# Macaron block on one core: paired slots in the first FFN, a shorter first stage, earlier scatters, and the last tables spread over half slots

## The chip, the cores and the metric

The kernel runs on one core of a Trainium2 chip. The metric is the device time of one execution in microseconds (us). Three timed executions of the kernel before gave 701.39, 701.4 and 705.12 us, with a median of 701.4 us. The profile is of one more execution.

## The reference

The input is x of shape (2, 2048, 256), so T = 4096 rows of D = 256, all float32. Three residual steps follow each other:

```
x = x + 0.5 * ffn(layernorm(x))
x = x + attn(layernorm(x))          # three gated linear recurrences, width 64, then up to 256
x = x + 0.5 * ffn(layernorm(x))     # the same weights again

def ffn(x, Wr, br, ln_g, ln_b, W1, b1, W2, b2):      # E = 8 experts, F = 1024
    logits = x @ Wr + br
    gate = max(softmax(logits)); idx = argmax(logits)     # one expert per row
    xn = layernorm(x) * ln_g + ln_b
    h = relu(xn @ W1[idx] + b1[idx])                      # 256 -> 1024
    return (h @ W2[idx] + b2[idx]) * gate                 # 1024 -> 256
```

Which rows go to which expert depends on the data. With the reference's router on its inputs (seed 0) the first FFN sends 332, 17, 1583, 15, 1969, 2, 0 and 178 rows to experts 0 to 7.

## The kernel before

**Slots.** Each FFN routes its rows: every row is written by an indirect DMA (a scatter, L743, GpSimd) into the region of its expert in DRAM (`routed_rows`), and is later read back in tiles of 128 rows of one expert. A tile is a slot. The work of a slot is: load 128 rows (`slot_rows`, SyncE) and the expert's W1 (`weights`, 1 MB); normalise on VectorE (`norm`, L1337); transpose on TensorE (`turn_input`, L1907); scale and shift on ScalarE (`affine`, L1626); first product (`first_product`, L1935, 16 products that the profile lists as 32 matmuls); bias and ReLU, half on ScalarE (L1654), half on VectorE (`activate`, L1369); second product (`second_product`, L1969, 16 matmuls listed); bias, gate and residual on VectorE (`finish`, L1387 and L1394); scatter of the result to its rows (`store`, L752, GpSimd).

**Software pipeline.** In the turn of slot i TensorE transposes slot i+1, runs the first product of slot i, then the second product of slot i-1. The order is written out by hand and is static. Two waits matter here. The second product of slot i-1 waits until VectorE has read all earlier second products, so on `finish(i-2)` (`m_yk`). The second half of the first product of slot i waits until VectorE has run `activate(i-1)` (`m_a`).

**Tables and stages.** Slot numbers are turned into row addresses and experts by tables that VectorE computes with small operations (`tables`, parts 0 to 5, after the counts of a quarter of the rows have come in). An FFN is cut into stages, so that it starts before all rows are routed. The first FFN has a stage of FULL = 9 slots (full tiles from the first half of the rows) and a second stage with all the rest. The second FFN has stages of 4, 9, 9 slots and the rest. A static number of slots, FIXED = 32, always runs; the ones behind that run under an `If` on the number of slots in use (`slots_used`). SLOTS = 39 is the upper bound in the first FFN.

**Paired slots.** A pair slot holds 64 rows of each of two experts (`is_pair`). The second FFN has three, at slots 24, 27 and 30; the first FFN has none. A pair needs two W1 loads and a second W2 (`pair_second_weights`, 1 MB into `w2_b`), has its first product the other way round (L1926), copies it out (L1349), transposes it back (`turn_hidden`, L1947), activates after that (`activate_pair`, L1357) and has a second product in two halves (L1961, L1963). VectorE chooses the experts (`pairs`, parts 0 to 2): experts with an odd number of half tiles come first.

**Work beside the slots.** Everything else (routing of the later quarters, tables, layer norms, the recurrences) stands in lists of positions k at the top of the file. Slot i has a place, `PLACE[p][i]`; in the first FFN that is i, plus 1 from the second stage on. `beside(at)` of VectorE, ScalarE and GpSimd runs what stands at k from 48*place to 48*place+23 ahead of the slot's activation, and at 48*place+24 to 48*place+47 behind it. For TensorE a place has 192 positions, in eight parts between the quarters of the products. Places go up to 39 in the first FFN whether or not a slot is in use: the work beside them is issued either way. `beside` work that is placed at slots 35 to 38 (places 36 to 39) is the first recurrence layer of the third quarter, the end of the recurrence of the second quarter (`up`, `add_recurrence` L1284, `moments` L856) and `turn_logits`. Chunk c of x is read back from `x_middle` (`load_x`) at slots 17, 23, 31 and after the last one (`WITH`).

**Engine order.** Each engine runs its own instructions in order. SyncE issues all loads in order: W1 of slot i+3, then rows of slot i+4; at a stage's first slot it waits for that stage's table (`s_tab`) and for the scatters.

## Time and profile before

| | |
|---|---|
| median of 3 timed executions | 701.4 us |
| profiled execution, its own time | 700.31 us |
| its span in the trace | 698.5 us |
| TensorE matmul busy | 642.4 us (92%) |
| VectorE busy | 412.0 us (59%) |
| ScalarE busy | 268.1 us (38%) |
| GpSimd busy | 168.6 us (24%) |
| slots run, first and second FFN | 37 and 34 (three of these are pairs) |

Busy time is the sum of an engine's spans; the share is of the span. The time that counts is that of the engine that the others wait for at each stretch, and that is read from the gaps ("idle before") and from what ended them.

### The profile page before, as it was taken

What the parts mean: (1) busy time and instruction counts of PE and PEld (TensorE: products, weight loads), DVE (VectorE), ACT (ScalarE), POOL (GpSimd) and SP (SyncE); (2) the same over time, 40 slices, a digit from 0 to 9 for tenths busy, and PEclk for the clock granted to TensorE, in tenths of its full rate; (3) what the DMA queues carried; (4) which work ended last, traced back from release to release, by engine and by line L of the source; (5) the groups of instructions that cost most, each with busy time, mean ns of one, the idle gap of its engine ahead of it and who ended that gap; (6) DMA issues with size and microseconds to landing.
All of it is one profiled execution on the core that took longest, in us unless ns stands there. A gap on an engine that the chain in (4) does not pass through costs nothing.

```text
span 698.5 us, 15261 instructions
## 1 busy us (share of the span) xinstructions
PE 642.4 (92%) x4294; PEld 550.9 (79%) x4294; DVE 412.0 (59%) x1446; ACT 268.1 (38%) x639; POOL 168.6 (24%) x174
## 2 busy tenths in 40 slices
PE   7549999999999999999998998999979899999993
PEld 5448988999988878898677867879878888786782
DVE  7756673333356586777787684877756762344331
ACT  4204221323245557553571644744442311233220
POOL 4633433111121120133312341104411331111111
PEclk9659999999999999999998999999999999999998
DMA  8969876845464463436415436434274445767640
GB/s 284 315 206 388 276 255 207 275 166 203 161 205 147 156 204 107 134 128 189 168 55 198 147 117 223 137 98 153 87 260 145 132 173 192 236 210 257 235 151 18
DMA packets 62512, 129.25 MB, mean 185 GB/s; under 512 B 8010, under 2 KB 39253, under 8 KB 62293
## 3 DMA queue, kind: packets, MB, share of 16 engines
q1 hardware_dynamic: 55940, 111.25, 47.8%
q0 software_dynamic: 6480, 16.92, 6.6%
q8 instruction: 41, 0.67, 0.4%
q14 instruction: 51, 0.41, 0.2%
HBM read 109.10 MB, written 19.96 MB: 185 GB/s over the span
## 4 chain that ended last, share of the span: by engine, by line
PE 63%; DVE 15%; issue 8%; DVEq 6%; POOL 3%; DMA 2%; ACT 1%; POOLq 0%; ACTq 0%; SPq 0%
PE bank L1935 27%; PE bank L1969 24%; PE bank L1907 2%; DVE st L856 2%; POOL routed_rows L743 2%; DVEq L454 2%; PE bank L1926 2%; PE bank L1961 2%; DVE rec L1253 1%; DVE act_t L1369 1%; DVE y_b L1387 1%; PE bank L1824 1%; DVE rec L1229 1%; PE bank L1831 1%; PE bank L1762 1%
## 5 line engine op out<-in xcount | busy, mean ns | idle before, releaser
L1935 PE MATMUL bank<-mn_t,w 128*128 128x128 f32 x2176 | 268.4, 280 | 8.3 <-DVE act_t L1369 4.7
L1935 PEld LDWEIGHTS bank<-mn_t,w 128*128 128x128 f32 x2176 | 258.1, 196 | 20.6 <-issue 11.5
L1969 PE MATMUL bank<-w,act_t 128*128 x1088 | 254.8, 383 | 5.7 <-DVE y_b L1387 5.3
L1969 PEld LDWEIGHTS bank<-w,act_t 128*128 128x128 f32 x1088 | 200.2, 191 | 43.0 <-issue 19.3
L1626 ACT ACTIVATE mn_t<-bank,vec 128x128 f32<-128x128 f32 x146 | 58.9, 456 | 224.2 <-PE bank L1907 224.2
L1369 DVE TENSOR_SCALAR act_t<-bank,vec 128x128 f32<-128x128 f32 x272 | 76.7, 345 | 80.2 <-PE bank L1935 66.7
L1654 ACT ACTIVATE act_t<-bank,vec 128x128 f32<-128x128 f32 x272 | 77.7, 368 | 61.3 <-PE bank L1935 61.1
L752 POOL DMA_INDIRECT x_middle<-res,pay x37 | 36.9, 999 | 217.1 <-DVE res L1394 176.7
L1387 DVE TENSOR_TENSOR y_b<-bank,b_all 128x256 f32<-128x256 f32 x68 | 28.9, 425 | 92.0 <-PE bank L1969 81.6
L752 POOL DMA_INDIRECT out_x<-res,pay x34 | 34.0, 999 | 197.2 <-DVE res L1394 153.0
L743 POOL DMA_INDIRECT routed_rows<-rows,dest x64 | 63.9, 998 | 58.0 <-PE bank L1935 28.2
L1337 DVE TENSOR_SCALAR mn<-pay 128x256 f32<-128x256 f32 x75 | 31.0, 415 | 28.1 <-DMA pay<-routed_rows 27.6
L735 POOL TENSOR_TENSOR inv_std<-var_eps,minus_half 128x16 f32<-128x16 f32 (+1 forms) x12 | 31.0, 2582 | 48.0 <-DVE var_eps L866 34.4
L1907 PE MATMUL bank<-ident,mn 128*128 128x128 f32 x146 | 29.2, 282 | 13.8 <-DVE mn L1337 9.8
L1394 DVE SCALAR_TENSOR_TENSOR res<-y_b,pay 128x256 f32<-128x256 f32 x71 | 34.4, 485 | 6.8
L1907 PEld LDWEIGHTS bank<-ident,mn 128*128 128x128 f32 x146 | 19.1, 143 | 22.9 <-issue 10.2
L856 DVE BATCH_NORM_STATS2 st<-rows 128x6 f32<-128x256 f32 x96 | 33.7, 414 | 2.7 <-DMA rows<-in_L_attn_h 0.8
L1229 DVE SCALAR_TENSOR_TENSOR rec<-seq,lay,rec 128x512 f32<-128x512 f32 x36 | 27.0, 749 | 2.0 <-issue 0.2
L1530 ACT ACTIVATE xn_t<-bank 128x512 f32<-128x512 f32 x32 | 17.7, 603 | 18.8 <-PE bank L1762 18.8
L1762 PE MATMUL bank<-ident,rows 128*128 128x128 f32 x128 | 20.3, 311 | 0.7 <-ACT xn_t L1530 0.6
L1568 ACT ACTIVATE rec<-bank,lay 64x512 f32<-64x512 f32 x24 | 16.4, 682 | 9.5 <-PE bank L1824 9.3
L1762 PEld LDWEIGHTS bank<-ident,rows 128*128 128x128 f32 x128 | 17.3, 164 | 3.4 <-issue 2.7
(249 smaller groups left out, 530.2 us busy)
## 6 DMA issues: line engine op xcount, KB each, us to landing
w<-in_L_ffn_W SPq DMA_DIRECT2D x82, 1024.0 KB, 5.3
pay<-routed_rows SPq DMA_DIRECT2D x72, 130.0 KB, 2.1
rows<-in_L_attn_h SPq DMA_DIRECT2D x8, 512.0 KB, 6.8
rows<-x_middle SPq DMA_DIRECT2D x8, 512.0 KB, 5.0
rec<-in_L_ffn_W SPq DMA_DIRECT2D x3, 1024.0 KB, 7.3
routed_rows<-fill SPq DMA_DIRECT2D x2, 1040.0 KB, 7.7
routed_rows<-rows,dest POOLq DMA_INDIRECT x64, 3.5
b_all<-in_L_ffn_b SPq DMA_DIRECT2D x1, 1024.0 KB, 11.5
```

The source lines that it names most:

```text
L743: g.indirect_dma_start(out=routed[f], out_offset=bass.IndirectOffsetOnAxis(ap=dest[:, t:t + 1], axis=0), in_=rows[:, t * RW:(t + 1) * RW], ...
L752: g.indirect_dma_start(out=x_out if p else x_mid, out_offset=bass.IndirectOffsetOnAxis(ap=pay[p][i % RING][:, C_ID:C_ID + 1].bitcast(I32), ...
L856: v.bn_stats(st[:, jj * 6:jj * 6 + 6], tile_of(c, b, j, 0, D))
L1369: last = v.tensor_scalar(act_t[i % 2][:, c * P:(c + 1) * P], b_hid[1][:, c % 4 * P:(c % 4 + 1) * P], vec[:, ds(eb + c, 1)], 0.0, ALU.add, ...
L1387: v.tensor_tensor(y_b[i % 2][:, :], b_out[i % 2], b2_all[:, ds(eb * (D // FC), D)], ALU.add).then_inc(m_yk[p], 1)
L1394: v.scalar_tensor_tensor(out=res[p][i % 2][:, :], in0=y_b[i % 2][:, :], scalar=a[:, C_GATE:C_GATE + 1], in1=a[:, 0:D], op0=ALU.mult, op1=A ...
L1626: last = a.activation(mn_t[p][i % 2][:, k * P:(k + 1) * P], b_in[i % 2][:, k * P:(k + 1) * P], ACT.Identity, scale=vec[:, V_G + k:V_G + k ...
L1654: last = a.activation(act_t[i % 2][:, c * P:(c + 1) * P], b_hid[0][:, c * P:(c + 1) * P], ACT.Relu, bias=vec[:, ds(eb + c, 1)])
L1762: last = t.transpose(bk[cc][n % 2][:, j * P:(j + 1) * P], tile_of(c, b, j, k * P, P), ident[:, :])
L1907: last = t.transpose(b_in[i % 2][:, k * P:(k + 1) * P], mn[p][i % 2][:, k * P:(k + 1) * P], ident[:, :])
L1935: last = t.matmul(b_hid[half][:, c % 4 * P:(c % 4 + 1) * P], w1[u % W1S][:, k * F + c * P:k * F + (c + 1) * P], mn_t[p][i % 2][:, k * P:(k ...
L1969: last = t.matmul(b_out[i % 2], act_t[i % 2][:, c * P:(c + 1) * P], w2[:, ds(eb * (WE // FC) + c * D, D)], start=c == 0, stop=c == FC - 1)
```

## The change

1. The first FFN gets two pair slots, at slots 11 and 14. `PAIRS`, `PAIR_AT`, the tables `pair_row`, `pair_b`, `pair_off` and the helpers take the FFN as an argument. ScalarE's `first_pass` calls `activate_pair`; SyncE's loads the W1 of pairs and the second W2.
2. The first stage of the first FFN has 8 slots in place of 9. The second stage starts at slot 8 (place 9; places of slots 9 and up stay as they are).
3. `pairs` for the first FFN is at k = 168, 168, 169 (place 3, behind the activation). Parts 0 to 4 of the second stage's tables stand at 192, 216, 240, 264, 288 in place of 169, 192, 240, 264, 288.
4. The scatters of the third and fourth quarter in the first FFN stand at 72 to 144 and 192 to 264, a half slot apart, in place of 72 to 216 and 264 to 408.
5. In the second FFN `pairs` is at 2880, 2904, 2905 in place of three times 2880, and the last tables at 2928, 2929, 2952, 2953, 2976 in place of 2881, 2904, 2905, 2952, 2953.

Upper bounds follow: SLOTS stays 39 in the first FFN and goes from 44 to 45 in the second; the last tables have 29 entries in the first FFN (30 before) and 20 in the second (19 before).

```diff
-R_SCATTER = [[[None, None, None, None], [None, None, None, None], [72, 120, 168, 216], [264, 312, 360, 408]],
+R_SCATTER = [[[None, None, None, None], [None, None, None, None], [72, 96, 120, 144], [192, 216, 240, 264]],
...
-TABLE_PARTS = [[[None, None, None, None, None, None], [169, 192, 240, 264, 288, None]], [[1584, 1609, 1633, 1682,
-    1683, 1728], [2066, 2088, 2112, 2113, 2116, 2281], [2497, 2544, 2568, 2569, 2593, 2616], [2881, 2904, 2905,
-    2952, 2953, None]]]
+TABLE_PARTS = [[[None, None, None, None, None, None], [192, 216, 240, 264, 288, None]], [[1584, 1609, 1633, 1682,
+    1683, 1728], [2066, 2088, 2112, 2113, 2116, 2281], [2497, 2544, 2568, 2569, 2593, 2616], [2928, 2929, 2952,
+    2953, 2976, None]]]
...
-PAIR_PARTS = [2880, 2880, 2880]
+PAIR_PARTS = [[168, 168, 169], [2880, 2904, 2905]]
...
-    PAIRS = 3
-    HALVES = 2 * PAIRS
-
-    EARLY = ((FULL,), (4, 9, 9))
+    PAIRS = (2, 3)
+
+    EARLY = ((FULL - 1,), (4, 9, 9))
...
-    TAKEN = (P * FULL, T - T // NC - PART)
-    LAST = [(T - TAKEN[0] + PART) // P, PAIRS + (T - TAKEN[1] + E * (HALF - 1)) // P]
+    TAKEN = (P * EARLY[0][0], T - T // NC - PART)
+    LAST = [PAIRS[p] + (T - t + E * (P - 1) - 2 * PAIRS[p] * HALF) // P for p, t in enumerate(TAKEN)]
...
-    PAIR_AT = [[], [FIRST[1][-1] + 2 + 3 * k for k in range(PAIRS)]]
-
-    WITH = (FULL + E, (TH + PART) // P, (T - T // NC + PART) // P)
+    PAIR_AT = [[FIRST[0][-1] + k for k in (3, 6)], [FIRST[1][-1] + k for k in (2, 5, 8)]]
+
+    WITH = (EARLY[0][0] + PAIRS[0] + E - 1, (TH + PART) // P, (T - T // NC + PART) // P)
...
                     if i + W1S < n:
                         with has_tile(sp, used if i + W1S >= FIXED[0] else None, 0, i + W1S):
-                            next_weights(0, i + W1S)
+                            weights_behind(0, i)
+                    if is_pair(0, i + 1):
+                        pair_second_weights(0, i + 1)
...
                     if i < FIXED[0]:
+                        if is_pair(0, i - 1):
+                            activate_pair(0, i - 1)
                         next_affine(0, i + 1)
...
-                    for part in range(3):
-                        if k == PAIR_PARTS[part]:
-                            pairs(part)
+                    for f in range(FFNS):
+                        for part in range(3):
+                            if k == PAIR_PARTS[f][part]:
+                                pairs(f, part)
```

## Rows read from the trace of the kernel before

**Rows 1.** The page, busy time of each engine over the whole span.

```profile
PE 642.4 (92%) x4294; PEld 550.9 (79%) x4294; DVE 412.0 (59%) x1446; ACT 268.1 (38%) x639; POOL 168.6 (24%) x174
```

**Rows 2.** The page, costliest groups: result scatters of the first FFN.

```profile
L752 POOL DMA_INDIRECT x_middle<-res,pay x37 | 36.9, 999 | 217.1 <-DVE res L1394 176.7
```

**Rows 3.** Busy time by stretch: each engine's busy us, granted clock, DMA share, GB/s.

```profile
60.00:124.00 64.00, 61.86 (x417) 56.77 (x417) 36.85 (x131) 14.99 (x47) 23.40 (x24) 1.00 0.78 265
124.00:196.00 72.00, 71.98 (x511) 67.61 (x510) 24.73 (x83) 21.40 (x66) 9.72 (x10) 1.00 0.61 207
...
349.00:378.00 29.00, 27.97 (x184) 22.79 (x180) 23.35 (x70) 14.81 (x29) 4.90 (x4) 1.00 0.40 147
...
560.20:562.00 1.80, 1.76 (x8) 1.76 (x9) 1.33 (x10) 0.00 (x0) 0.00 (x0) 0.52 0.53 216
```

**Rows 4.** Timeline of TensorE, plain slots (start, duration; idle before in brackets).

```profile
141.75 0.38 PE L1907 MATMUL bank<-ident,mn 128*128 128x128 f32 x2
...
148.99 0.38 PE L1907 MATMUL bank<-ident,mn 128*128 128x128 f32 x2
```

**Rows 5.** Timeline of TensorE, second FFN: the transposes that open each third slot.

```profile
605.21 0.38 PE L1907 MATMUL bank<-ident,mn 128*128 128x128 f32 x2
...
628.33 0.38 PE L1907 MATMUL bank<-ident,mn 128*128 128x128 f32 x2
...
652.25 0.38 PE L1907 MATMUL bank<-ident,mn 128*128 128x128 f32 x2
...
676.01 0.38 PE L1907 MATMUL bank<-ident,mn 128*128 128x128 f32 x2
```

**Rows 6.** Timeline of VectorE, second FFN: starts of the parts of pairs and tables.

```profile
551.28 0.17 DVE L978 TENSOR_TENSOR seg_x<-cnt,done 128x8 f32<-128x8 f32 x1
...
553.39 0.17 DVE L996 TENSOR_SCALAR seg_end<-seg_pre 128x8 f32<-128x8 f32 x1
...
555.01 0.21 DVE L1011 TENSOR_TENSOR beyond<-jump,e_desc 128x48 f32<-128x48 f32 x1
...
556.70 0.17 DVE L1064 TENSOR_TENSOR seg_x<-cnt,done 128x8 f32<-128x8 f32 x1
```

**Rows 7.** Timeline of TensorE, second FFN, around the last tables.

```profile
554.96 1.95 PE L1935 MATMUL bank<-mn_t,w 128*128 128x128 f32 x16
560.24 3.67 PE L1935 MATMUL bank<-mn_t,w 128*128 128x128 f32 x16 [3.33 <-DVE act_t L1369]
...
574.88 0.38 PE L1907 MATMUL bank<-ident,mn 128*128 128x128 f32 x2
```

**Rows 8.** Timeline of VectorE, first FFN, slots 3 to 5 (finish of slots 2 and 4).

```profile
80.65 0.19 DVE L1064 TENSOR_TENSOR seg_x<-cnt,done 128x32 f32<-128x32 f32 x1
...
83.53 0.42 DVE L1387 TENSOR_TENSOR y_b<-bank,b_all 128x256 f32<-128x256 f32 x1 [0.81 <-issue]
...
85.32 0.58 DVE L1337 TENSOR_SCALAR mn<-pay 128x256 f32<-128x256 f32 x1 [0.79 <-DMA pay<-routed_rows]
...
98.87 0.42 DVE L1387 TENSOR_TENSOR y_b<-bank,b_all 128x256 f32<-128x256 f32 x1
```

**Rows 9.** Timeline of TensorE, first FFN, places 4 to 6.

```profile
84.45 3.62 PE L1969 MATMUL bank<-w,act_t 128*128 x16
...
91.39 2.05 PE L1935 MATMUL bank<-mn_t,w 128*128 128x128 f32 x16 [1.32 <-DVE act_t L1369]
...
100.53 3.62 PE L1969 MATMUL bank<-w,act_t 128*128 x16
```

**Rows 10.** Timeline of TensorE, end of the first FFN (places 36 to 38).

```profile
349.11 0.44 PE L1907 MATMUL bank<-ident,mn 128*128 128x128 f32 x2
...
354.18 1.12 PE L1831 MATMUL bank<-rec,rec_t 128*128 128x512 f32 x2 [0.62 <-DVE rec L1253]
...
370.47 1.04 PE L1790 MATMUL bank<-pick,lg_t 128*128 128x16 f32 x8
...
379.19 0.52 PE L1907 MATMUL bank<-ident,mn 128*128 128x128 f32 x2 [1.60 <-DVE mn L1337]
```

More of the change, by code:

```diff
@@ L278, in macaron_block, with words @@
         later = sb("later", [P, LATER], I32)
[L279 to L285 removed]
+        WORDS = [[sum(COUNT[p])] * 3 + [2 * PAIRS[p]] * 2 + [PAIRS[p], 1] for p in range(FFNS)]
+        tab = sb("tab", [P, sum(map(sum, WORDS))], I32)
+        def words(p, n):
+            at = sum(map(sum, WORDS[:p])) + sum(WORDS[p][:n])
+            return tab[:, at:at + WORDS[p][n]]
+        tab_row, tab_b, tab_off, pair_row, pair_b, pair_off, tab_used = (
+            [words(p, n) for p in range(FFNS)] for n in range(7))
         pay = [[sb(f"pay{i}_{s}", [P, RW]) for s in range(RING)] for i in range(2)]
@@ L631, in between_passes @@
                         for i in range(W1S):
-                            last = max(j for j in range(u) if j % W1S == i)
-                            sp.wait_ge(m_h[0], 2 * last + 2)
+                            last = max(j for j in range(u) if any(load % W1S == i for load in loads_of(0, j)))
+                            sp.wait_ge(m_h[0], halves_before(0, last) + 2)
                             next_weights(1, i)
@@ L966, in keep_counts, with pairs @@
                 dve.drain()
-            def pairs(part):
+            def pairs(f, part):
+                n = 2 * PAIRS[f]
                 every = cnt_c[:, NC - 1, :]
@@ L972, in pairs @@
                 order = beyond_s[:, 0:E * E].rearrange("p (e k) -> p e k", e=E)
-                of = jump_s[:, 0:HALVES * E].rearrange("p (h e) -> p h e", e=E)
-                of_row = beyond_s[:, E * E:E * E + HALVES * E].rearrange("p (h e) -> p h e", e=E)
-                row, short, by = (a[:, 0:HALVES] for a in (slot_v, slot_c, slot_r))
-                sq, of_all = [P, E, E], [P, HALVES, E]
+                of = jump_s[:, 0:n * E].rearrange("p (h e) -> p h e", e=E)
+                of_row = beyond_s[:, E * E:E * E + n * E].rearrange("p (h e) -> p h e", e=E)
+                row, short, by = (a[:, 0:n] for a in (slot_v, slot_c, slot_r))
+                sq, of_all = [P, E, E], [P, n, E]
                 if part == 0:
@@ L1037, in tables @@
                 i0 = FIRST[f][s]
-                slots = i0 + PAIRS if f and last else i0
+                slots = i0 + PAIRS[f] if last else i0
                 rw, tb, of = (t[f][:, i0:i0 + n] for t in (tab_row, tab_b, tab_off))
@@ L1340, in norm @@
                 if is_pair(p, i):
-                    n = PAIR_AT[1].index(i)
-                    off = pair_off[:, n:n + 1]
+                    n = PAIR_AT[p].index(i)
+                    off = pair_off[p][:, n:n + 1]
                 else:
@@ L1351, in activate_pair @@
             def activate_pair(p, i):
-                experts = [expert_of_half(dve, i, h) for h in range(2)]
+                experts = [expert_of_half(dve, p, i, h) for h in range(2)]
                 dve.wait_ge(m_h[p], halves_before(p, i) + 4)
@@ L1374, in finish @@
                 if is_pair(p, i):
-                    experts = [expert_of_half(dve, i, h) for h in range(2)]
+                    experts = [expert_of_half(dve, p, i, h) for h in range(2)]
                     dve.wait_ge(m_y[p], i + 1)
@@ L1634, in activate_pair @@
             def activate_pair(p, i):
-                experts = [expert_of_half(act, i, h) for h in range(2)]
+                experts = [expert_of_half(act, p, i, h) for h in range(2)]
                 act.wait_ge(m_h[p], halves_before(p, i) + 3)
```

55 lines of the change are left out of this document (24 added, 31 removed).

## The prediction

> **What bounds the kernel now.** I read the page first. TensorE has matmuls in flight for 92% of the span, VectorE for 59% [rows 1], so a stretch is TensorE's unless a gap shows otherwise. The share doesn't say which stretch the change touches, so I went by stretches and then by the timelines. From 124 to 196 us TensorE is busy 71.98 of 72 us: plain slots, nothing beside them, 148.99 - 141.75 = 7.24 us each [rows 3, 4]. From 60 to 124 us it is busy 61.86 of 64, with VectorE at 36.85: nearly full, but VectorE carries routing and tables there, and at 91.39 TensorE has waited 1.32 us for an activation [rows 3, 9]. In the second FFN the same kind of wait is 3.33 us at 560.24, and the 16 matmuls behind it take 3.67 us where 16 take 1.95 [rows 7], since the granted clock is 0.52 there, the 1.2 GHz level, after full clock [rows 3]. The end of the first FFN, 349 to 378 us, has TensorE busy 27.97 of 29 us and VectorE 23.35, so both are close to being the bound [rows 3]. The change touches all four kinds of stretch; I take its effects one by one.
>
> **Slots.** x_middle is scattered 37 times [rows 2], which is the sum of the tiles of 128 over the experts' counts: 3+1+13+1+16+1+0+2 = 37. In half tiles the counts are 6, 1, 25, 1, 31, 1, 0, 3: six experts are odd. Four halves go to experts 1 to 4, each of which saves a tile: 8 + 2 pairs + 25 (2, 0, 9, 0, 11, 1, 0, 2) = 35 slots. So two slots go, 2 x 7.24 = 14.5 us of TensorE at the plain price. That is not the gain: the slots that go are the last two, at places 36 and 37, and the work beside them stays.
>
> **End of the first FFN: -2.5 us.** The stretch from the opening of place 36 to the first transpose of the second FFN is 379.19 - 349.11 = 30.1 us [rows 10]. Without slots 35 and 36 it holds the second product of slot 34 and the work beside. Its length is then VectorE's: of the 23.35 us that VectorE is busy there [rows 3] two normalisations, two activations and two finishes go, 2 x (0.5 + 1.1 + 0.9) = 5.0, and 18.3 us stay. That is the floor, a gain of up to 10 us. But they are one chain with the other engines in it: scan, rescale, ScalarE's tap, convolution, TensorE's gates, ScalarE's tanh and exp, gate input, root, scan, second moments, first normalisation of the next FFN. TensorE already waits for the scan at 354.18 [rows 10]. Laying the chain out from there with today's durations and no matmuls between, the second moments end some 5 us earlier than today. Against this, TensorE now idles about 4 us ahead of the scan's projection and about 4 us ahead of `turn_logits` (370.47 today, rows 10), and both bursts then run at half clock as at 560.24: each makes some 1.7 us of matmuls 1.7 us longer (3.67 - 1.95) [rows 7], and projection, gates and `turn_logits` are on the chain. I take half of the 5 us: -2.5. Bounds: -5 (clock stays) and +0.5 (both bursts in full, and one more wait behind them). Nobody waits there for DMA: W1 for the next FFN no longer waits for slot 36.
>
> **Two pairs: +3.8 us.** From 605.21 to 676.01 the second FFN runs nine slots with three pairs in 70.80 us [rows 5]; nine plain ones are 65.2 [rows 4]. That is 5.6 / 3 = 1.9 us a pair, and the pairs at slots 11 and 14 stand in the stretch in which TensorE has no gap at all [rows 3], so both count in full: 3.8. Bounds 2.6 to 4.6: the three pairs differ between 1.4 and 2.2 (23.9 us for the slots from 628.33, 23.8 from 652.25). The number of W1 loads stays at 37, two W2 loads of 1 MB come in on SyncE's queue, at a DMA share of 0.61 [rows 3].
>
> **Pairs on VectorE at place 3: +4.0 us, and +0.5 for the clock.** `pairs` takes 556.70 - 551.28 = 5.42 us for six halves [rows 6]; with four halves its operations are a little smaller, with the same number. It now stands behind the activation of slot 3 and ahead of finish(2), and nothing hides it: between 80.65 and 98.87 VectorE's only breaks are 0.8 us gaps at register loads and one wait of 0.79 us for rows [rows 8]. So finish(2) goes from 83.53 to about 86.9, while TensorE wants it at 84.45 for the second product of slot 3 [rows 8, 9]: an idle of about 2.9 us. It catches up a little and waits again, about 2.5 us, behind part 1 of the tables, that now stands behind the activation of slot 4. Finish(4) goes from 98.87 to about 104.1 (+5.42, less 0.79 of waiting, plus a new gap); the second product of slot 5 that starts at 100.53 now [rows 9] starts at 104.5. From there VectorE has nothing beside and TensorE is the bound: +4.0 (bounds 3.4 and 5.4). The 1.32 us at 91.39 go, and are in this. Whether the two idles take the clock down: 1.32 us did not (16 matmuls in 2.05), 3.33 us did [rows 7, 9]. If only the first does, it is hidden under the second wait; if the second does, it is 1.7. I put 0.5.
> The Trainium skill (TensorE: Matmul & The Clock Gate, Why this matters for your kernels) asks that TensorE have no long idle between bursts, or it falls back to half clock, here at both gaps; by that the term would be 1.7 in place of 0.5. The row at 560.24 agrees with it, and no row here has an idle of just this length ahead of busy matmuls.
>
> **First stage of eight slots, earlier scatters: 0.** The places of slots 9 and up stay, so the break between stages costs what it does, a slot earlier. The table is now done at about 106 (part 4 behind finish(4)). SyncE stands at W1 of slot 8 until then, and behind it in its queue are W1 of slot 9 and the rows of slots 8 and 9, wanted at about 118: 5 to 10 us of slack. The eight scatters move ahead of that; GpSimd is busy 23.40 of 64 us there [rows 3] and each is about 1.3 us, so the stores stay within a slot; they move the same bytes at a DMA share of 0.78. I bound the edit by -0.8 (a wait for rows at the break goes) and +2 (W1 lands late behind the denser scatters) and take 0: every load has over a slot of lead.
>
> **Last tables in halves: -3.0 us.** Today pairs (5.42) and part 0 of the tables stand ahead of one activation, and TensorE waits 3.33 us for it, then runs 16 matmuls 1.72 us too long [rows 7]. From 554.96 to the slot opened at 574.88 it is 19.9 us for what takes 14.3 without gaps (two slots of 7.24 less the transposes, 14.48 - 0.22): 5.6 lost. Now only part 0 of `pairs` (2.11 = 553.39 - 551.28) is ahead of that activation, which is over at 555.3, before TensorE wants it at 556.8. Parts 1 and 2 (1.62 and 1.69, rows 6) come behind it and ahead of a finish, which is ready at 559.8 and wanted at 558.5: 1.3 us of idle. Tables 0 and 1 then delay the next activation by about 1.0, and the next finish by 0.3. Together 2.6 in place of 5.6, none long enough for the clock: -3.0. Bounds: -4.5 and -1.0. The table itself is done some 3 us later, four slots ahead of its stage; behind SyncE's wait for it stand loads for slot 22 that also wait for matmuls of that time. The 20th entry costs nothing that shows.
>
> **Sum.** -2.5 + 3.8 + 4.0 + 0.5 + 0 - 3.0 = +2.8 us on the profiled execution's 700.31 (its span is 698.5, with 1.8 us around it), so 703.1. The median of the runs is 701.4, 1.1 above that execution; +2.8 on it is 704.2. That is 0.4% slower. A measurement of this kernel can tell about 0.5%, or 3.5 us, so faster begins below 697.9 and slower above 704.9.
>
> **The rivals.**
> A. The two slots come off in full. If matmuls were what fills 349 to 378 us (27.97 of 29 speaks for it), the end would give 10 us, VectorE's floor, in place of 2.5: 704.2 - 7.5 = 696.7; with the early wait half hidden too, 694. Against it: the chain with ScalarE in it, and the wait at 354.18 that is there already [rows 3, 10]. Chance 0.14.
> B. VectorE's lists cost less than I count: the early delay at 3.4, clock kept at both gaps at the end (-5), pairs at 1.4 each, tables -3.5. That is 3.4 + 2.8 - 5 - 3.5 = -2.3, so 699.1. Chance 0.14.
> C. The clock takes the gain, and the change is slower. Place: the bare places 36 to 38 and the two early idles. Price: 1.72 us a burst [rows 7]; two early and two late on top of the chain make the early term 5.7 and the end 0: 5.7 + 3.8 + 0 - 3.0 = +6.5, so 707.9. It decides as soon as idles under 3 us take the clock down; the rows have 1.3 us that don't and 3.3 us that do. Chance 0.18. The rule of the Trainium skill cited above (TensorE: Matmul & The Clock Gate) would make it this one.
> D. The pairs save no slot (the odd experts are not chosen first, 37 plus 2 slots in use less those two): the end keeps its 30.1 us, +4.5 + 3.8 - 3.0 = +5.3, 706.7. The counts speak against it. Chance 0.04.
> The forecast has 0.50, of which 0.28 lies within 0.5% and 0.22 above it (its own range 701 to 707.5). Faster: A, 0.14. Same: 0.28 + B 0.14 = 0.42. Slower: 0.22 + C 0.18 + D 0.04 = 0.44. The range takes in B, C and D and leaves most of A out: 698.5 to 709.5.
>
> **What would show it.** Of the profile after: x_middle scattered 35 times, out_x 34. Ahead of the second products of slots 3 and 4, waits of TensorE for y_b (L1387) of 2 to 3 us, and the second product of slot 5 near 104.5. The slots with L1926 at 11 and 14 at +1.9 each. In the bare places a span of about 27 us with TensorE idle two times for 3 us or more, and a granted clock of about 0.5 behind each. Around 555 us (plus the shift of some 5 us) three short waits in place of one of 3.33, at full clock. I am wrong if finish(2) isn't late, which means that VectorE had room; if the bare places take 20 us or less; or if SyncE's loads for slot 8 land after TensorE wants them.

## The result and the profile after

| | before | after |
|---|---|---|
| median | 703.3 us (4 runs) | 715.3 us (4 runs, 709.4 to 717.5) |
| ratio, 95% interval | | 1.0147, 1.0093 to 1.0201 |
| profiled execution, span | 700.31, 698.5 us | 713.11, 711.3 us |
| granted TensorE clock, mean of that execution | 0.967 | 0.941 |

The change is 1.5% slower. The forecast was 704.2 us, its range ended at 709.5: wrong by 11 us. A second measurement of the same kernel (below) gave 1.0147 again. Part of the 11 us is the baseline: the forecast started from three runs with a median of 701.4, and later medians of the kernel before, over 17 to 29 runs, are 702.8 to 704.6. The change itself costs 1.47% of 703, 10.3 us, where I had summed 2.8.

The page after, busy time and result scatters [rows 1, 2]:

```profile
PE 641.3 (90%) x4210; PEld 539.3 (76%) x4210; DVE 413.0 (58%) x1467; ACT 266.8 (38%) x637; POOL 166.7 (23%) x172
...
L755 POOL DMA_INDIRECT x_middle<-res,pay x35 | 34.8, 995 | 218.8 <-DVE res L1399 191.8
L755 POOL DMA_INDIRECT out_x<-res,pay x34 | 33.9, 996 | 197.8 <-DVE res L1399 137.1
```

Two slots went (35 in place of 37), as counted. TensorE is busy for 1 us less in a span 12.8 us longer; its busy time also counts matmuls that take twice as long at the lower clock. Busy time by stretch, after [rows 3]; the last two lines are the end of the first FFN, some 12 us later than before:

```profile
60.00:124.00 64.00, 58.55 (x380) 52.13 (x379) 39.11 (x155) 13.84 (x43) 23.24 (x23) 0.97 0.77 262
124.00:196.00 72.00, 71.30 (x498) 59.38 (x496) 27.76 (x92) 21.66 (x70) 8.88 (x9) 1.00 0.74 252
349.00:378.00 29.00, 23.44 (x128) 15.94 (x128) 19.36 (x61) 15.75 (x26) 6.62 (x6) 0.88 0.41 151
378.00:406.00 28.00, 21.75 (x118) 18.85 (x119) 18.22 (x69) 10.40 (x23) 3.49 (x2) 0.63 0.24 77
```

The early stretch has 5.5 us of TensorE idle (2.1 before); the end has 5.6 and 6.3 us of idle at a clock of 0.88 and 0.63, where TensorE had been busy 27.97 of 29 us at 1.00.

**Early places.** Timelines of TensorE, VectorE and ScalarE after [rows 8, 9]:

```profile
91.11 5.40 PE L1976 MATMUL bank<-w,act_t 128*128 x16 [3.04 <-DVE y_b L1392]
...
101.54 3.72 PE L1976 MATMUL bank<-w,act_t 128*128 x16 [1.24 <-DVE y_b L1392]
...
108.89 3.40 PE L1976 MATMUL bank<-w,act_t 128*128 x15
```

```profile
79.15 0.43 DVE L1392 TENSOR_TENSOR y_b<-bank,b_all 128x256 f32<-128x256 f32 x1 [2.53 <-remote]
...
84.29 0.17 DVE L982 TENSOR_TENSOR seg_x<-cnt,done 128x8 f32<-128x8 f32 x1
...
90.44 0.42 DVE L1392 TENSOR_TENSOR y_b<-bank,b_all 128x256 f32<-128x256 f32 x1 [0.81 <-issue]
```

```profile
79.13 0.81 ACT L1631 ACTIVATE mn_t<-bank,vec 128x128 f32<-128x128 f32 x2 [5.65 <-remote]
```

The same operation of ScalarE in the kernel before:

```profile
73.72 0.81 ACT L1626 ACTIVATE mn_t<-bank,vec 128x128 f32<-128x128 f32 x2 [2.70 <-PE bank L1907]
```

The wait of 3.04 us for finish(2), behind `pairs` (84.29 to 89.6), is the one foretold as 2.9; the matmuls behind it take 5.40 us for 3.62. The second wait, foretold as about 2.5 us, is the 1.24 at 101.54. The second product of slot 5 starts at 108.89, not at 104.5. What wasn't foretold is at 79 us: ScalarE stands 5.65 us and VectorE 2.53 us. The profile puts both waits down to "remote", which means that no instruction ended close to the moment at which the semaphore was raised. The trace of before has no such row at all. (The trace's own records of these semaphores say more; see "Open".)

**End of the first FFN.** Timeline of TensorE after [rows 10]:

```profile
365.77 2.07 PE L1838 MATMUL bank<-rec,rec_t 128*128 128x512 f32 x2 [2.82 <-DVE rec L1257]
367.63 3.62 PE L1976 MATMUL bank<-w,act_t 128*128 x8
...
383.59 1.86 PE L1797 MATMUL bank<-pick,lg_t 128*128 128x16 f32 x8 [3.82 <-DVE rows L1288]
385.29 1.87 PE L1801 MATMUL bank<-up_r,rec 128*128 128x16 f32 x8
386.99 2.05 PE L1838 MATMUL bank<-rec,rec_t 128*128 128x512 f32 x2
...
392.04 0.67 PE L1914 MATMUL bank<-ident,mn 128*128 128x128 f32 x2
```

From the scan's projection to the first transpose of the second FFN it is 26.3 us after and 25.0 before (354.18 to 379.19): no gain. The projection takes 2.07 us for 1.12, the 8 matmuls of the last second product 3.62 for 1.97, `turn_logits` 3.73 for 2.08: all at the 1.2 GHz level, behind idles of 2.82 and 3.82 us.

**Last tables.** Timeline of TensorE after [rows 7]:

```profile
575.78 3.71 PE L1976 MATMUL bank<-w,act_t 128*128 x16 [0.84 <-DVE y_b L1392]
...
581.98 2.05 PE L1942 MATMUL bank<-mn_t,w 128*128 128x128 f32 x16 [0.48 <-DVE act_t L1374]
584.62 3.72 PE L1976 MATMUL bank<-w,act_t 128*128 x16 [0.58 <-DVE y_b L1392]
```

Three short waits at full clock in place of one of 3.33 us at half, as forecast.

**Where the time went**, in the profiled executions: each column is how much longer a stretch is than in the kernel before, from the starts of the rows of VectorE's `res` (L1394, after L1399), one a slot. "Start" is the finish of slot 0; the last column is slots 15 to 19 of the second FFN.

| kernel | start | slots 0 to 9 | 9 to 17 | 33 to first of second FFN | second FFN, 15 to 19 |
|---|---|---|---|---|---|
| after | 2.5 | 5.7 | 3.7 | 1.1 | -2.5 |
| after, measured again | 4.1 | 9.3 | 4.1 | -0.9 | -2.5 |
| last tables only | 1.9 | -0.2 | 0.0 | 0.0 | -2.2 |
| stage and scatters | 1.9 | 4.2 | 0.0 | -1.1 | 1.2 |
| scatters only | 2.7 | 3.9 | 0.0 | -1.1 | 0.0 |
| third quarter's scatters only | 2.8 | 1.2 | 0.0 | 0.0 | 1.0 |
| stage only | 2.9 | 5.3 | 0.0 | -1.1 | 1.1 |
| changed, pairs spread | 1.7 | 7.8 | 3.9 | -0.9 | -2.5 |
| changed, scatters to 360 | 3.0 | 10.3 | 3.3 | 0.1 | -2.5 |
| changed, scatters to 312 | 3.1 | 6.1 | 6.6 | -0.6 | -2.5 |
| changed, nine slots, read at 18 | 2.1 | 4.2 | 3.6 | -0.6 | -2.5 |
| changed, nine slots, read at 17 | 4.0 | 4.4 | 3.8 | 0.9 | -2.5 |
| changed, clock kept | 3.0 | 6.3 | 3.4 | -4.8 | -2.5 |
| changed, nine slots, clock kept | 3.2 | 3.9 | 4.3 | -3.8 | -2.6 |
| the same, pairs spread | 3.5 | 5.9 | 3.0 | -3.7 | -2.6 |

The column "start" isn't the change: the kernel with the last tables alone, whose first FFN is that of before, has it too. The profiled execution of before was a lucky one there, so traces differ by 1.7 to 4.1 us more than the medians do. ScalarE's rows of before and after show where:

```profile
31.05 0.24 ACT L1505 ACTIVATE vec<-bank 128x83 f32<-128x83 f32 x1 [5.57 <-PE bank L1744]
```

```profile
42.15 0.24 ACT L1510 ACTIVATE vec<-bank 128x83 f32<-128x83 f32 x1 [16.44 <-remote]
```

Every other trace has this operation at 42.0 to 42.8 us, behind a "remote" wait of 12.5 to 16.4 us. The sixteen scatters of the first two quarters, issued in a row from 19.3 to 38.7 us, stand ahead of it in all of them, in that of before too. So the one trace that I forecast from is the one without this stall.

Single executions scatter by some 4 us; the verdicts below go by ratios over 5 rounds.

### The profile page after: what moved, and what is told of

The parts are those of the page before. It is cut to its first block, busy times and chain, and to the rows that moved or that the text cites. A ratio compares the mean times of both kernels' runs of the same rounds, so it can differ in the third digit from the quotient of the medians.

```text
span 711.3 us, 15098 instructions
## 1 busy us (share of the span) xinstructions
PE 641.3 (90%) x4210; PEld 539.3 (76%) x4210; DVE 413.0 (58%) x1467; ACT 266.8 (38%) x637; POOL 166.7 (23%) x172
## 4 chain that ended last, share of the span: by engine, by line
PE 60%; DVE 17%; DVEq 8%; issue 8%; another core or an unknown queue 3%; ACT 2%; POOL 1%; DMA 1%; POOLq 0%; ACTq 0%
PE bank L1942 23%; PE bank L1976 21%; PE bank L1933 3%; PE bank L1968 2%; DVEq L455 2%; PE bank L1914 2%; DVE st L859 2%; DVE act_t L1374 1%; DVE y_b L1392 1%; PE bank L1838 1%; PE bank L1831 1%; PE bank L1769 1%; PE bank L1843 1%; DVE rec L1257 1%
## 5 line engine op out<-in xcount | busy, mean ns | idle before, releaser
L1942 PE MATMUL bank<-mn_t,w 128*128 128x128 f32 x2048 | 251.4, 279 | 3.9 <-ACT mn_t L1631 1.9
L1976 PE MATMUL bank<-w,act_t 128*128 x1024 | 244.4, 388 | 11.2 <-DVE y_b L1392 10.8
L1942 PEld LDWEIGHTS bank<-mn_t,w 128*128 128x128 f32 x2048 | 241.8, 195 | 15.8 <-issue 10.9
L1976 PEld LDWEIGHTS bank<-w,act_t 128*128 128x128 f32 x1024 | 191.2, 194 | 50.1 <-issue 26.9
L1374 DVE TENSOR_SCALAR act_t<-bank,vec 128x128 f32<-128x128 f32 x256 | 72.1, 344 | 69.1 <-PE bank L1942 53.1
L1659 ACT ACTIVATE act_t<-bank,vec 128x128 f32<-128x128 f32 x256 | 73.1, 368 | 56.3 <-PE bank L1942 56.2
L755 POOL DMA_INDIRECT x_middle<-res,pay x35 | 34.8, 995 | 218.8 <-DVE res L1399 191.8
L1392 DVE TENSOR_TENSOR y_b<-bank,b_all 128x256 f32<-128x256 f32 x64 | 27.1, 424 | 91.2 <-PE bank L1976 75.8
L1399 DVE SCALAR_TENSOR_TENSOR res<-y_b,pay 128x256 f32<-128x256 f32 x69 | 33.4, 484 | 6.7
L1914 PEld LDWEIGHTS bank<-ident,mn 128*128 128x128 f32 x142 | 18.9, 146 | 14.1 <-issue 10.3
L1797 PE MATMUL bank<-pick,lg_t 128*128 128x16 f32 x64 | 10.2, 294 | 15.8 <-ACT lg_t L1544 12.0
L1797 PEld LDWEIGHTS bank<-pick,lg_t 128*128 128x128 f32 x64 | 10.1, 236 | 18.4 <-ACT lg_t L1544 13.8
```

What stands on the lines that cost most here:

```text
L755: g.indirect_dma_start(out=x_out if p else x_mid, out_offset=bass.IndirectOffsetOnAxis(ap=pay[p][i % RING][:, C_ID:C_ID + 1].bitcast(I32), ...
L1374: last = v.tensor_scalar(act_t[i % 2][:, c * P:(c + 1) * P], b_hid[1][:, c % 4 * P:(c % 4 + 1) * P], vec[:, ds(eb + c, 1)], 0.0, ALU.add, ...
L1392: v.tensor_tensor(y_b[i % 2][:, :], b_out[i % 2], b2_all[:, ds(eb * (D // FC), D)], ALU.add).then_inc(m_yk[p], 1)
L1399: v.scalar_tensor_tensor(out=res[p][i % 2][:, :], in0=y_b[i % 2][:, :], scalar=a[:, C_GATE:C_GATE + 1], in1=a[:, 0:D], op0=ALU.mult, op1=A ...
L1659: last = a.activation(act_t[i % 2][:, c * P:(c + 1) * P], b_hid[0][:, c * P:(c + 1) * P], ACT.Relu, bias=vec[:, ds(eb + c, 1)])
L1914: last = t.transpose(b_in[i % 2][:, k * P:(k + 1) * P], mn[p][i % 2][:, k * P:(k + 1) * P], ident[:, :])
```

## The experiments

The first four, on one chip with the same runs of before (median 703.8):

**Last tables alone.** Before, with `PAIR_PARTS` and the last row of tables as changed:

```diff
-    2952, 2953, None]]]                                 # last tables at 2881, 2904, 2905, 2952, 2953
+    2953, 2976, None]]]                                 # 2928, 2929, 2952, 2953, 2976
-PAIR_PARTS = [2880, 2880, 2880]
+PAIR_PARTS = [2880, 2904, 2905]
```

> The kernel before with one edit: pairs and last tables of the second FFN in halves (2880, 2904, 2905 and 2928 to 2976). In the two traces, the shift between them shrinks by 2.8 us across these tables. Theory W (the waits on VectorE): the 3.33 us wait of TensorE near 557 us becomes three short ones, and the time falls by 2.5 to 3 us. Rival L (the layout: every edit moves the code and the DMA times, and the waits at code fetch and at loads move by microseconds): the local gain shows in the trace, but the time moves by anything from -4 to +4 us.

701.8 us, 0.9960 (0.9933 to 0.9987). By the ratio a gain of 2.8 us where I had put 3.0 (the medians are 1.9 apart). This is the one version whose interval lies below the kernel before.

**Stage and scatters alone.** Before, with both rows of scatters, the first part of the tables at 192, and:

```diff
-    EARLY = ((FULL,), (4, 9, 9))
+    EARLY = ((FULL - 1,), (4, 9, 9))
```

> The kernel before with the first stage of eight slots, the scatters a half slot apart, and part 0 of the second stage's tables at 192; no pairs in the first FFN (37 slots), the last tables as before. Theory W: 0, within 1 us of the kernel before; part 0 of the tables moves behind the finish of slot 2, and the activation of slot 4 comes some 2 us later, which may add up to 1.5 us. Rival S (the stage and the scatters are what costs): 3 us or more slower, with TensorE waiting for W1 or rows of slot 8, or for loads delayed by the scatters.

711.5 us, 1.0105 (1.0059 to 1.0151). The edit that I costed at 0 costs 7.4 us by itself. Its trace has ScalarE standing at 78.51 us for 5.64 and again at 93.49 for 6.59, both "remote".

**The changed kernel with its pairs spread.**

```diff
-PAIR_PARTS = [[168, 168, 169], ...
+PAIR_PARTS = [[168, 192, 193], ...        # tables at 216 to 312
```

> The changed kernel with the pairs of the first FFN in halves (168, 192, 193) and its tables a half slot later (216 to 312). Theory W: the waits of 3.0 us (second product of slot 3) and 1.2 us shrink to about 2 us in all, the clock stays at full there; 3.5 to 4.5 us faster than the changed kernel. Rival L: the local waits go, but the time against the changed kernel moves by no more than 1 us or goes up, since other waits take their place.

714.2 us, 1.0134 (1.0095 to 1.0172): not told from the changed kernel, where I had expected 3.5 to 4.5 us. The density of `pairs` isn't where the 11 us are. Its trace has ScalarE standing 8.39 us until 81.12 and 7.25 until 96.90, both "remote", so this edit was tried underneath the stalls.

**The changed kernel again**, without an edit.

> The changed kernel once more, unedited. In its first trace ScalarE, VectorE and SyncE stall between 30 and 42 us (gaps of 1.1 us between small operations of VectorE, ScalarE idle 16.4 us), 3.4 us until the first slot, and rows for slot 4 of the second FFN come 2 us later than their issue explains. Theory C (chance of one execution): the first slot opens at 45 to 46 us as before, and the profiled time is 3 us or more below 713. Rival L (layout): both delays are there again in place and size, with the time at 713 to 717.

714.0 us, 1.0147 (1.0102 to 1.0193). The stall that ends at 42 us is there again (ScalarE 15.10 us), the profiled execution took 713.8 us, and the wait of ScalarE near 80 us is there too (7.02 us, at 82.13), so neither is a chance of one execution. A late load of rows for slot 4 of the second FFN (VectorE waits 5.87 us in the first trace) isn't there: that one is.

**Which half of the stage-and-scatters edit.** Four kernels on one chip (before 702.8). First the scatters alone, in the kernel before:

```diff
-... [72, 120, 168, 216], [264, 312, 360, 408]],
+... [72, 96, 120, 144], [192, 216, 240, 264]],
```

> The kernel before with the closer scatters alone (72 to 144, 192 to 264); first stage of nine slots, tables as before. Measured so far: stage and scatters together cost 1.05% (+7.4 us). Theory G (the scatters, issued back to back on GpSimd, fill its DMA queue and hold up the loads and the other engines' instructions between 78 and 97 us): this kernel has the cost, 709 to 711 (+5.5 to +7.5), with waits of VectorE and ScalarE near 79 us as in that kernel. Theory T (the break between stages, a slot earlier, meets work that isn't ready): 703.5 to 704.5 (0 to +1).

707.3 us, 1.0057 (1.0029 to 1.0084): +4.0 us, less than theory G's 5.5 to 7.5 and well more than theory T's 0 to 1, with the waits that theory G asked for. GpSimd and ScalarE of this run:

```profile
73.29 0.97 POOL L743 DMA_INDIRECT routed_rows<-rows,dest  x1 [0.30 <-issue]
74.56 0.98 POOL L743 DMA_INDIRECT routed_rows<-rows,dest  x1 [0.30 <-issue]
75.84 0.98 POOL L743 DMA_INDIRECT routed_rows<-rows,dest  x1 [0.30 <-issue]
77.13 0.97 POOL L743 DMA_INDIRECT routed_rows<-rows,dest  x1 [0.30 <-issue]
```

```profile
79.19 0.81 ACT L1626 ACTIVATE mn_t<-bank,vec 128x128 f32<-128x128 f32 x2 [5.52 <-remote]
83.74 1.14 ACT L1654 ACTIVATE act_t<-bank,vec 128x128 f32<-128x128 f32 x4 [3.74 <-remote]
```

Each entry of the list issues two scatters, 1.28 us apart. Four scatters stand in a row ahead of the stall; in the trace of before there are two, then a store and two more, and ScalarE's operation starts at 73.72 right after the transpose.

Then the stage alone, with the scatters a whole slot apart and their last one as far ahead of the new break as it was of the old:

```diff
-    EARLY = ((FULL,), (4, 9, 9))
+    EARLY = ((FULL - 1,), (4, 9, 9))
-... [72, 120, 168, 216], [264, 312, 360, 408]],
+... [72, 120, 168, 216], [240, 288, 336, 360]],
```

> The kernel before with a first stage of eight slots and scatters a whole slot apart (72 to 216, then 240 to 360, so that the last stands as far ahead of the new break as it did); tables as before, no pairs. Theory G: 703.5 to 705 (0 to +1.5). Theory T: 708.5 to 711.5 (+5 to +7.5), with the loss at the break, places 8 to 10.

709.0 us, 1.0066 (1.0033 to 1.0098). The loss is at the break, as theory T had it, and its rows say why. VectorE and TensorE of this run:

```profile
119.94 0.41 DVE L1337 TENSOR_SCALAR mn<-pay 128x256 f32<-128x256 f32 x1 [3.74 <-DMA pay<-routed_rows]
```

```profile
115.86 1.99 PE L1969 MATMUL bank<-w,act_t 128*128 x8 [1.45 <-issue]
120.45 0.41 PE L1907 MATMUL bank<-ident,mn 128*128 128x128 f32 x2 [2.60 <-issue]
```

The last scatter was issued at 114.42 and the rows of slot 8 were asked for at 117.89. TensorE stands 1.45 us and then 2.60 us, the second time until those rows are in, and the 8 matmuls that follow take 3.43 us where 8 take 1.89 in the kernel before. No ScalarE wait near 80 us. So each half costs, by two different waits, and I had priced neither.

The changed kernel with those spread scatters (72 to 216, 240 to 360):

> The kernel after with its scatters a whole slot apart (72 to 216, 240 to 360). All else as in the change. Theory G: it wins back what the scatters cost, 706.5 to 709 (changed kernel 714). Theory T: 713 to 715, no difference from the changed kernel. If pairs on VectorE at place 3 and the scatters hide each other in part (both hold up the same turn), it lies between, 709 to 712.

715.4 us, 1.0157 (1.0115 to 1.0198). Nothing won: the early stall goes and the late rows of slot 8 come (finish(6) to finish(7) takes 9.4 us, 4.8 in the changed kernel). Theory G alone, which asked for 706.5 to 709, falls.

The changed kernel with nine slots in the first stage and the scatters of before (pairs now at slots 12 and 15):

> The kernel after with a first stage of nine slots (pairs at slots 12 and 15) and the scatters where they stood before (72 to 216, 264 to 408): pairs, first-FFN tables and last tables of the change without its stage and scatters. By the terms that the traces bear out (pairs +3.7, pairs on VectorE +4, last tables -2.5, end of the first FFN -2.5 to +1): 706.5 to 710. Theory T and theory G both give this; a theory that the pairs and not the stage or the scatters cost what is missing gives 713 to 715.

718.5 us, 1.0217 (1.0182 to 1.0252), a miss by all theories. Its slots 0 to 9 are 4.2 us longer and 9 to 17 3.6, but slots 17 to 19 another 7.4. TensorE and SyncE of this run:

```profile
214.14 1.97 PE L1769 MATMUL bank<-ident,rows 128*128 128x128 f32 x8 [5.18 <-DMA rows<-x_middle]
```

```profile
209.83 0.93 SPq L505 DMA_DIRECT2D rows<-x_middle  x2
```

My edit had moved the first read-back of x (`WITH`) from slot 17 to 18 through the formula, and TensorE waited 5.18 us for it: a fault of the experiment.

**Scatters that avoid both waits.** Four kernels on one chip (before 703.9). The changed kernel, then the stage-only kernel, each with:

```diff
+... [72, 120, 168, 216], [240, 264, 288, 312]],
```

> The kernel after with the third quarter's scatters a whole slot apart (72 to 216) and the fourth's half a slot apart but later (240, 264, 288, 312). Measured so far: with all scatters closer, ScalarE waits 5 to 8 us near 80 us; with them spread to 360 the rows of slot 8 arrive late and the break costs 4.6 us. Theory G (each of these two is a cost of its own): both go, 709.5 to 711.5 (changed kernel 714 to 715), no such ScalarE wait near 80 us and slot 9 at about +9 instead of +13.3 (kernel with scatters to 360). Theory P (pairs on VectorE at place 3 set the time of the early places whatever the scatters do): 712.5 to 714.5.

712.3 us, 1.0120 (1.0085 to 1.0155): below the changed kernel, short of what theory G asked for, and the intervals overlap. Both waits are gone from its trace (no stall near 80 us, finish(6) to finish(7) 4.8 us, slot 9 at +9.1), and two others have come. VectorE of this run:

```profile
113.11 1.12 DVE L1374 TENSOR_SCALAR act_t<-bank,vec 128x128 f32<-128x128 f32 x4 [4.27 <-remote]
...
164.78 0.41 DVE L1342 TENSOR_SCALAR mn<-pay 128x256 f32<-128x256 f32 x1 [3.65 <-DMA pay<-routed_rows]
```

The first stands behind the fourth quarter's scatters, which are again four in a row here (109.14 to 112.97). The second is a late load of rows: finish(11) to finish(12) takes 10.8 us, 7.9 in the changed kernel, and slots 9 to 17 cost 6.6 us in place of 3.7.

> The kernel before with a first stage of eight and the scatters at 72 to 216 and 240 to 312; no pairs, tables as before. Theory G: the edit that I costed at 0 is then near 0: 703 to 705 (against +7.4 with all scatters closer, +4.6 with them spread to 360). If the break itself costs more a slot earlier: 706 to 709.

704.3 us, 0.9993 (0.9968 to 1.0018). By these times a stage of eight costs nothing that shows, if the scatters are neither four in a row near 73 us nor late for the break. (Its profiled execution, 712.4 us, is far above that median; no row of it is used, so which waits are gone is not shown here.)

The nine-slot kernel with the read-back at slot 17:

```diff
-    WITH = (EARLY[0][0] + PAIRS[0] + E - 1, ...
+    WITH = (EARLY[0][0] + PAIRS[0] + E - 2, ...
```

> The kernel after with nine slots in the first stage and the scatters where they stood before, as in the earlier run (718.5), but with the first read-back of x at slot 17 in place of 18. In that run slot 18 finished 6.2 us later than slot 17 would have it, and slot 19 7.4. Theory R (the recurrence waits for the read-back, a slot later): 710.5 to 712.5, slots 18 and 19 at about +10 instead of +16 and +17. Otherwise 717 to 719.

710.2 us, 1.0080 (1.0054 to 1.0106), as theory R had it (0.3 us under its range; slots 18 and 19 at +12.2). This is the changed kernel without its stage-and-scatters edit: that edit is worth 1.0147 - 1.0080 = 0.67%, 4.7 us, inside the change. The intervals of these two ratios just touch; with the clock kept (below) the same edit is worth 0.65%, and there they lie apart.

**The clock at the end of the first FFN.** The changed kernel, with TensorE kept at work in the bare places (written for 35 slots in use):

```diff
+            KEEP = {6960: 12, 7104: 8, 7368: 19, 7440: 5}
+            def keep_busy(n):
+                pe.wait_ge(m_a[0], 35)
+                for _ in range(n):
+                    t.matmul(b_hid[1][:, 0:P], ident[:, :], ident[:, :], start=True, stop=True)
...
+                    if k in KEEP:
+                        keep_busy(KEEP[k])
```

> The kernel after with 44 matmuls of 128 columns whose results are never read, put ahead of TensorE's waits in the bare places of the first FFN (12 ahead of the scan's projection, 8 ahead of the second up-projection, 19 ahead of turn_logits, 5 ahead of the last norms). Theory C (the half clock takes what the two slots leave): granted clock 1.0 from 362 to 392 us, the stretch from finish(34) to the first finish of the second FFN 4 to 6 us shorter, 708.5 to 711. Theory H (the chain through ScalarE and VectorE takes it, the clock is beside it): 0 to 1 us shorter, 713 to 715.

710.7 us, 1.0077 (1.0052 to 1.0101). Stretches of this kernel, then of the changed one:

```profile
360.00:370.00 10.00, 8.71 (x57) 5.65 (x53) 8.01 (x21) 3.48 (x6) 1.04 (x1) 1.00 0.67 218
370.00:380.00 10.00, 9.57 (x72) 7.33 (x72) 7.07 (x21) 5.70 (x7) 0.98 (x1) 1.00 0.56 210
380.00:390.00 10.00, 8.09 (x64) 7.13 (x63) 7.61 (x29) 2.88 (x6) 2.94 (x1) 1.00 0.21 72
```

```profile
360.00:370.00 10.00, 6.13 (x22) 3.33 (x21) 8.02 (x20) 3.59 (x6) 1.05 (x1) 0.76 0.67 249
370.00:380.00 10.00, 7.91 (x43) 5.21 (x42) 4.57 (x17) 5.70 (x7) 0.97 (x1) 0.84 0.33 132
380.00:390.00 10.00, 5.46 (x18) 3.91 (x18) 8.21 (x25) 1.55 (x3) 2.02 (x1) 0.50 0.36 106
```

And TensorE of this kernel, against the rows at 365.77, 367.63 and 383.59 above:

```profile
366.74 1.12 PE L1838 MATMUL bank<-rec,rec_t 128*128 128x512 f32 x2
367.77 1.99 PE L1985 MATMUL bank<-w,act_t 128*128 x8
...
377.99 4.51 PE L1874 MATMUL bank<-ident 128*128 128x128 f32 x38 [0.43 <-issue]
382.33 0.96 PE L1797 MATMUL bank<-pick,lg_t 128*128 128x16 f32 x8
383.14 1.04 PE L1801 MATMUL bank<-up_r,rec 128*128 128x16 f32 x8
384.04 1.10 PE L1838 MATMUL bank<-rec,rec_t 128*128 128x512 f32 x2
```

The granted clock is 1.00 in these stretches and the same work takes about half as long. The stretch from finish(33) to the first finish of the second FFN is 42.0 us (before 46.7, after 47.8 and, measured again, 45.8). From finish(34), as I had put it, it is 3.0 us shorter than in the changed kernel's first trace, less than the 4 to 6 expected. The time is in theory C's range. More TensorE work, less time: theory C.

**Do the two causes add up?** Three kernels on one chip (before 704.6). Nine slots, read-back at 17, and the unread matmuls:

> The kernel after with nine slots in its first stage, the scatters where they stood before, the read-back at slot 17 (710.2, ratio 1.0080), and the 44 unread matmuls in the bare places (which alone took the changed kernel from 714 to 710.7). If the two causes add: 704 to 707. If the second only mends what the first made late: 709 to 711.

705.1 us, 1.0012 (0.9985 to 1.0039). They do: 0.67% and 0.70% alone, 1.35% together, of the 1.47%. What is left is not told from the kernel before.

The same, with less at once on VectorE:

```diff
-PAIR_PARTS = [[168, 168, 169], ...        # tables at 192 to 288
+PAIR_PARTS = [[168, 192, 216], ...        # tables at 240 to 336
```

> As the run before it, with the parts of pairs for the first FFN at 168, 192, 216 in place of 168, 168, 169, and its tables at 240 to 336 in place of 192 to 288, so that VectorE never has more than one of them ahead of a finish. Theory V (pairs and tables on VectorE at places 3 to 5 cost the 4.3 us seen from slot 0 to slot 9, and part of it is their density): 2 to 3 us less than the run before it, 702 to 704. If the table is then late for the loads of slot 9: 1 us less to 2 us more, 704 to 708, with TensorE waiting at places 9 and 10.

704.6 us, 0.9997 (0.9968 to 1.0027). Not told from the run before it. Its trace shows both halves of the second theory: slots 0 to 4 are 3.0 us longer than before in place of 4.6, and the break gives it back; SyncE issues the first W1 loads of the second stage at 115.48 in place of 110.75, and slot 8 finishes 3.8 us later relative to slot 7.

The kernel before, with the third quarter's scatters alone closer (72, 96, 120, 144):

> The kernel before with the third quarter's scatters alone half a slot apart (72, 96, 120, 144); the fourth's stay at 264 to 408. With both closer it measured 1.0057. Theory G3 (the four scatters in a row near 73 us hold up the engines): 706.5 to 708.5, ratio near 1.005, ScalarE waiting 5 us or more near 79 us. Theory G34 (the sum of eight in 12 half slots, so that the queue never empties): 703 to 705, ratio 0.999 to 1.002.

707.4 us, 1.0035 (1.0010 to 1.0060). ScalarE of this run:

```profile
79.46 0.81 ACT L1626 ACTIVATE mn_t<-bank,vec 128x128 f32<-128x128 f32 x2 [5.63 <-remote]
```

Theory G3: the four in a row bring the stall. They cost 0.35%, both quarters 0.57%, but the intervals overlap, so the share of the fourth quarter stays open.

Over all traces: each of the seven kernels or repeats with the third quarter's four scatters in a row has a "remote" wait of ScalarE, 5.5 to 8.4 us long, that ends between 78 and 84 us; none of the nine others used here has one in that stretch. Behind the fourth quarter's scatters it is less regular. Where they are four in a row, ScalarE stands 6.59 us until 93.49 (stage and scatters), 6.33 until 98.24 (scatters only), 7.25 until 96.90 (changed, pairs spread), and VectorE 4.27 until 113.11 (changed, scatters to 312). The changed kernel in both its traces, the one with the clock kept, the stage-only kernel (110.59 to 114.42) and the changed kernel with scatters to 360 have four in a row there too, and no such wait of 2 us or more behind them. So four in a row alone don't decide it.

## Why the prediction was wrong

**First stage of eight slots, earlier scatters: 0.** This step failed. "Every load has over a slot of lead", and bounds of -0.8 and +2, were argued from SyncE's queue and a DMA share of 0.78 [rows 3]. Measured: 7.4 us alone, 4.7 inside the change. It is the one term that came out clearly beyond its bounds. I asked when the scattered rows and the table were needed, and in the kernel after they are in time. I counted GpSimd's issue time for the stores only, and that at half: "each is about 1.3 us" holds for one scatter, but each of the eight entries issues two, 2.56 us, so two entries half a slot apart come out as four scatters in a row. I did not count at all what four indirect DMAs in a row near 73 us go with on engines that never touch them: ScalarE stands 5.65 us, VectorE 2.53. No row of before has four in a row near 73 us, so the upper bound had no measurement behind it. The only longer burst in that trace, sixteen in a row from 19.3 us, shows no stall, and all sixteen other traces have one there. The idea of the edit was sound with other positions (0.9993).

**End of the first FFN: -2.5.** The mechanism was right, the size wrong. It measured between -0.9 and +1.1 in the seven traces with pairs and no unread matmuls. Kernels without pairs in the first FFN, which keep all 37 slots, have -1.1 to 0.0 (the three at -1.1 are those in which the wait of some 1.6 us ahead of the first transposes is followed by full clock). So two slots less gave nothing. I had laid out the chain (5 us) and halved it for the clock. The chain was right: with the clock kept the stretch is 3.7 to 4.8 us shorter. The clock costs nearly all of it, not half. At 1.2 GHz the whole burst is slow, and I counted 1.7 us a burst where there are two projections, half a second product and both parts of `turn_logits`: 2.07 + 3.62 + 1.86 + 1.87 + 2.05 is 11.5 us for what takes 6.2 in the kernel with the clock kept (1.12 + 1.99 + 0.96 + 1.04 + 1.10). The Trainium skill (TensorE: Matmul & The Clock Gate, Why this matters for your kernels), which I had set aside for 0.5 us and named under rival C, asks for no long idle between bursts; idles of 2.82, 3.04 and 3.82 us in the kernel after are each followed by matmuls at the lower level, one of 1.24 is not, so these rows agree. But the length of the idle alone doesn't decide it. TensorE of the changed kernel with nine slots and the read-back at 18, and of the kernel before:

```profile
89.62 3.72 PE L1976 MATMUL bank<-w,act_t 128*128 x16 [2.90 <-DVE y_b L1392]
```

```profile
379.19 0.52 PE L1907 MATMUL bank<-ident,mn 128*128 128x128 f32 x2 [1.60 <-DVE mn L1337]
```

An idle of 2.90 us is followed by 16 matmuls at full clock here (in the nine-slot kernel with the clock kept, one of 2.41 us at the same product is followed by 16 in 5.29 us), and one of 1.60 us by the lower level (a granted clock of 0.50 from 380 to 385 us; the same wait in the scatters-only kernel, at 385.72, is followed by full clock). The row of 1.60 us was in rows 10. So "1.32 us did not, 3.33 us did" read too little from my own rows, and rival C's condition, that idles under 3 us take the clock down, had a case for it before the run.

**Two pairs: +3.8.** Right: slots 9 to 17 take 61.65 us (205.15 less 143.50) for 57.98, +3.7; 3.0 to 4.3 in eight other traces, and 6.6 in the one with the late load of rows at 164.78.

**Pairs on VectorE: +4.0 and +0.5.** Right in size: where neither a scatter stall nor the shorter stage lies over it, slots 0 to 9 are 3.9 to 4.4 us longer. The wait of 3.04 did take the clock down in the kernel after; the second wait, 1.24 us for the 2.5 foretold, did not.

**Last tables: -3.0.** Right: -2.2 to -2.6 in every trace that has the edit, 2.8 by the ratio of the kernel that has them alone.

**Sum.** With 0 for the end in place of -2.5, the kernel without stage and scatters should cost +5.3 by my own terms; it measured 5.6 (0.80%). The rest is the failed step. Of the rivals C was nearest in mechanism (the clock takes the gain), and still 7 us short of the median (4 of them once the baseline is taken out: +6.5 for the measured 10.3), since no rival touched the scatters. Its price, 1.72 a burst, was that of 16 matmuls.

**Open.** What holds the engines up. The input was there by the rows: in the scatters-only kernel the transposes that ScalarE's operation at 79.19 reads ended at 76.33. The trace also records when each semaphore is raised, and that narrows it. That operation waits for one semaphore alone, which those transposes of TensorE raise, and it was raised at 79.16, 2.8 us after their recorded end. In the kernel after, the second product that VectorE waits for ended at 75.86 and its semaphore was raised at 79.02; the transposes ended at 76.17, theirs at 79.11. ScalarE and VectorE start 0.02 and 0.13 us behind. In the trace of before each semaphore that these two wait for follows TensorE's matmuls by 0.01 to 0.02 us. In all seven traces with the stall near 80 us its semaphore is one of TensorE's, raised 2.8 to 5.7 us after the recorded end of its matmuls, and the stall that ends at 42 us is the same: an operation of TensorE recorded as ended at 29 to 32 us, its semaphore at 42.0 to 42.7. So ScalarE and VectorE were ready, and what came late was the end of TensorE's work or the signal of it. Which of the two, the traces can't tell, since the ends of matmuls are modelled; nor what in the scatters brings it about, or why it comes near 73 us each time and behind the fourth quarter only at times.

That instructions arrive late behind the scatters' transfers is only argued, and for ScalarE and VectorE these records speak against it. The view of the DMA queues has one packet of an "instruction" queue between 76 and 77 us both in the kernel after, which stalls, and in the one with the last tables alone, which doesn't. The Trainium skill (Runtime: NRT & Kernel Launch, Instruction fetch mechanics) says that an engine fetches its instructions in blocks over a DMA queue of its own and that this is mostly hidden; no run here shows whether it was late for TensorE. Why the changed kernel gains less from better scatter positions (1.0120) than the kernel before does is told in part by its trace, which has the stall at 113.11 and the late rows at 164.78; that other executions have them is not shown.

## What to carry to other kernels

Work taken off a bound engine in a stretch that a chain of other engines nearly fills buys idle time, and on TensorE that idle can cost clock: price the whole burst behind it at half speed (here 11.5 us for 6.2), or keep the engine at work with matmuls that nobody reads. The spacing of indirect DMAs had a price here on engines that don't use them (0.57% in the scatters-only kernel); a trace that shows them only two at a time bounds nothing for four, and one trace of a kernel can be the lucky one. When a profile names no releaser, look at which semaphore the operation waits for and who raises it. When a formula ties a transfer to a stage's size, look where the transfer lands before comparing.

## What the runs showed that was not expected

- Four scatters in a row near 73 us, 1.28 us apart, go with a stall of ScalarE of 5.5 to 8.4 us in seven of seven traces; with two and two, and a store between, there is none in nine. The semaphore that ends it is TensorE's, and comes 2.8 to 5.7 us after the recorded end of the matmuls that raise it.
- 44 products of 128 columns whose results nobody reads make the changed kernel 0.70%, 4.9 us, faster (1.0147 to 1.0077).
- A read-back of x one slot later cost 7.4 us in slots 17 to 19 of the trace, and 1.0217 against 1.0080 in the ratios.
- An idle of TensorE of 2.90 us left the clock at full, one of 1.60 us was followed by half clock.
